# Moving the second-half query work and the routing tables inside two narrow attentions of a four-layer transformer kernel

## The reference

```
x = x + xattn0(LN(x), ctx)    # 8 heads of 16        "a0"
x = x + moe0(LN(x))           # top 2 + shared       "f0"
x = x + xattn1(LN(x), ctx)    # 8 heads of 128       "a1"
x = x + moe1(LN(x))           # top 2                "f1"
x = x + xattn2(LN(x), ctx)    # 16 heads of 8, mask  "a2"
x = x + moe2(LN(x))           # top 2                "f2"
x = x + xattn3(LN(x), ctx)    # 16 heads of 8, bias  "a3"
x = x + moe3(LN(x))           # top 1                "f3"
```

## Time and profile before

| | us |
|---|---|
| median of 3 executions (lowest, highest) | 915.8 (913.2, 916.91) |
| profiled execution, its time | 914.47 |
| profiled execution, its span | 912.7 |
| PE busy | 747.1 (82%) |
| DVE busy | 483.6 (53%) |
| ACT busy | 374.2 (41%) |
| POOL busy | 138.8 (15%) |
| mean granted TensorE clock, share of full speed | 0.903 |

### The profile page before, as it was taken

The page is one execution under the profiler, slowest core; times in us unless marked ns, Lnnn a source line. Parts: engine busy times, 40 slices in busy tenths (PEclk is TensorE's granted clock), DMA queues, the critical chain, the costliest instruction groups (busy, mean ns, idle before and its releaser), DMA issues.

```text
span 912.7 us, 14542 instructions
## 1 busy us (share of the span) xinstructions
PE 747.1 (82%) x5219; PEld 575.4 (63%) x5219; DVE 483.6 (53%) x1477; ACT 374.2 (41%) x768; POOL 138.8 (15%) x282
## 2 busy tenths in 40 slices
PE   3157899999998998799398936999999995898367
PEld 2025588887774666689387813676798982454266
DVE  6355574353325558766755325665655436576423
ACT  1024654433334554553243303556443331565234
POOL 7021130000000001013500001111000003123124
PEclk9568999999999999989799957999999996799679
DMA  4729930001254545990003623113001531323253
GB/s 118 137 37 277 152 95 1 1 24 50 63 179 137 164 159 150 206 202 10 1 1 72 68 34 57 52 52 98 1 1 46 73 56 33 50 77 86 71 152 153
DMA packets 78164, 77.49 MB, mean 85 GB/s; under 512 B 10849, under 2 KB 69237, under 8 KB 78094
## 3 DMA queue, kind: packets, MB, share of 16 engines
q1 hardware_dynamic: 77230, 74.99, 37.0%
q0 software_dynamic: 864, 1.58, 0.5%
HBM read 46.65 MB, written 28.78 MB: 83 GB/s over the span
## 4 chain that ended last, share of the span: by engine, by line
PE 60%; DVE 15%; DMA 11%; SPq 4%; issue 4%; POOL 3%; ACT 2%; POOLq 0%; DVEq 0%; ACTq 0%
PE bank L1692 15%; PE bank L1424 13%; PE bank L1512 4%; DMA big<-parts_scratch 4%; DVE xn L620 3%; PE bank L1495 3%; PE bank L1460 3%; DMA parts_scratch<-big 3%; SPq L344 3%; PE bank L1776 3%; PE bank L1809 2%; DMA big<-nmT 2%; PE bank L1651 1%; PE bank L1676 1%; DVE x_res L977 1%
## 5 line engine op out<-in xcount | busy, mean ns | idle before, releaser
L1692 PEld LDWEIGHTS bank<-W,late 128*128 128x128 f32 x1600 | 185.8, 192 | 8.3 <-issue 4.1
L1692 PE MATMUL bank<-W,late 128*128 128x128 f32 x1600 | 186.5, 275 | 0.0
L977 DVE SCALAR_TENSOR_TENSOR x_res<-bank,comb,x_res 128x128 f32<-128x128 f32 x200 | 56.3, 344 | 167.5 <-PE bank L1692 165.8
L1266 ACT ACTIVATE late<-bank,b 128x512 f32<-128x512 f32 x136 | 91.9, 688 | 95.2 <-PE bank L1424 94.3
L742 DVE TENSOR_REDUCE negmax<-bank 128x2 f32<-128x512 f32 x128 | 85.6, 689 | 84.2 <-PE bank L1460 56.6
L1460 PE MATMUL bank<-big 128*128 128x256 bf16 x320 | 74.4, 310 | 55.1 <-DMA big<-parts_scratch 42.5
L1424 PE MATMUL bank<-nH,wH 128*128 128x512 f32 x200 | 88.9, 445 | 2.5 <-DVE nL L780 2.4
L1195 ACT ACTIVATE late<-bank 128x512 f32<-128x512 f32 x120 | 70.6, 594 | 48.3 <-PE bank L1500 22.3
L1495 PE MATMUL bank<-big 128*128 128x256 bf16 x320 | 76.7, 290 | 11.9 <-DMA big<-nmT 10.2
L1460 PEld LDWEIGHTS bank<-big 128*128 128x128 bf16 x320 | 29.5, 107 | 84.9 <-issue 53.2
L1424 PE MATMUL bank<-nH,wL 128*128 128x512 f32 x200 | 81.3, 407 | 0.0
(11 more groups left out here) (269 smaller groups left out, 1278.2 us busy)
## 6 DMA issues: line engine op xcount, KB each, us to landing
W<-in_f_w SPq DMA_DIRECT2D x50, 256.0 KB, 3.5
rows_scratch<-zrow SPq DMA_DIRECT2D x1, 9252.0 KB, 54.4
late<-bands_scratch SPq DMA_DIRECT2D x8, 1024.0 KB, 5.8
big<-parts_scratch SPq DMA_DIRECT2D x18, 256.0 KB
big<-parts_scratch SPq DMA_DIRECT2D x36, 128.0 KB
W<-in_f_wx SPq DMA_DIRECT2D x8, 512.0 KB, 3.8
big<-in_f_wx SPq DMA_DIRECT2D x7, 578.0 KB, 6.9
bands_scratch<-late SPq DMA_DIRECT2D x3, 1276.0 KB, 6.6
```

What stands on the lines that cost most here:

```text
L977: ins = v.scalar_tensor_tensor(x[:, t, :], bank[4 + u % 2][:, 128 * i:128 * (i + 1)], comb[:, t, e:e + 1], x[:, t, :], ALU.mult, ALU.add)
L1266: ins = a.activation(dst, bank[c][:, :], func, bias=b1[:, bi, FC * e + c:FC * e + c + 1])
L1692: ins = mm(dst[:, 128 * i:128 * (i + 1)], hid[u % 2][:, c, 128 * i:128 * (i + 1)], W[:, e, F + 128 * c:F + 128 * (c + 1)], start=c == 0, s ...
```

## The change

The steps of the second half of the queries are tied to SECOND_HALF: unchanged for a0 (1), for a2 and a3 statistics in step 12, scaling in 13, transposes and matmul in 15, parts in 18. SyncE stores the second half ahead of the maxima of group 4 and loads it behind them. Experts are loaded one behind each of groups 6 to 13. On GpSimd the maxima parts of groups 0 to 2 go ahead of the layer norm a2.1 or a3.1. The tables are built after the layer norm f2.1, inside the mixture f2, and the row numbers (two iotas) apart from them, before the first rows are sent.

```diff
+SECOND_HALF = {"a0": 1, "a2": 12, "a3": 12}
...
                 stack(key, 0, 0)
-                maxima_to_rows(key, 0)
-                stack_out(key, 0, 1)
-                maxima_to_rows(key, 1)
-                stack_in(key, 0, 1)
-                for g in range(2, 16):
+                for g in range(16):
+                    if g == 4:
+                        stack_out(key, 0, 1)
                     maxima_to_rows(key, g)
-                    if g >= 4 and g % 2 == 0:
-                        expert(nxt, g // 2 - 2)
-                for e in range(6, 8):
-                    expert(nxt, e)
+                    if g == 4:
+                        stack_in(key, 0, 1)
+                    if g >= 6:
+                        expert(nxt, g - 6) if g < 14 else None
...
-            def route_tables():
+            def row_numbers():
 
                 pool.wait_ge(*at("f2", "down", 16))
                 pool.wait_ge(*at("f1", "acc", 16))
...
                 for hf in range(2):
                     ins = pool.iota(sends[hf][:, :, 2 * D:ROWW].bitcast(i32), pattern=[[128, 4], [0, 1]], base=512 * hf, channel_multiplier=1)
                 ins.then_inc(sem("f3.ids"), 1)
+
+            def route_tables():
+
+                pool.wait_ge(*at("f1", "acc", 16))
...
             for name in norms:
                 if name == "a1.0":
                     wide_tables()
+                if name in ("a2.1", "a3.1"):
+                    maxima_parts(name[:2], range(3))
                 layer_norm_rstd(name)
...
-                if name in ("a0.1", "a2.1", "a3.1"):
-                    maxima_parts(name[:2], range(0, 8 if name == "a0.1" else 2))
-                if name == "a3.1":
+                if name == "a0.1":
+                    maxima_parts("a0", range(8))
+                if name == "f2.1":
                     route_tables()
                 if name in ("a2.1", "a3.1"):
-                    maxima_parts(name[:2], range(2, 13))
+                    maxima_parts(name[:2], range(3, 13))
                 if name in ("f2.0", "f3.0"):
                     maxima_parts(BEFORE[name[:2]], range(13, 16))
+                if name == "f3.0":
+                    row_numbers()
...
+                start = SECOND_HALF[key]
...
-                    if i == 1:
+                    if i == start:
                         x_ready(dve, key, 1)
                         norm_stats(key, 1, x)
-                    if i == 2:
+                    if i == start + 1:
                         norm_apply(key, 1, x, xn)
-                    if i == 7:
+                    if i == start + 6:
                         query_parts(key, 1)
...
-                    if i == 4:
+                    if i == SECOND_HALF[key] + 3:
                         copy_T(key, 1, nT[0])
                         queries(key, 1)
...
-                    if i == 4:
+                    if i == SECOND_HALF[key] + 3:
                         turn_norm(key, 1)
                         queries(key, 1)
```

## The result

| | before | after |
|---|---|---|
| median of 4 executions (lowest, highest), us | 916.36 (913.2, 921.35) | 905.5 (905.16, 908.19) |
| profiled execution, span, us | 912.7 | 903.9 |
| mean granted TensorE clock | 0.903 | 0.913 |

The account below looks back on a forecast made before the run. The prediction took the attentions' steady parts as full, with starts waiting on second-half work, tables and maxima transfers. Gains of 4.0 us (a2) and 1.0 (a3) took the median from 915.8 to 910.8 us, range 904 to 918.

Parts of the forecast that it names:

- Step 11 after a start without query work: Start of a2 and a3: without second-half work step 11 comes earlier, 6.4 us gained in a2 and 7.7 in a3.
- The assumed flight of the first maxima: Start of both attentions: transfer takes 2.5 to 3 us, no wait; at 4.8 us both starts lose together 4.3.
- The moved work in the full part: Query work put into steps 12 to 18: costs 3.9 us in a2 and 7.7 in a3.
- The stop moves: PE's wait for maxima moves from step 19 to step 31: stops of 5.5 us in a2 and 7.6 in a3.
- The tables: Start of a3: building them in f2 takes PE's 2.81 us wait out of the path to step 16.
- Low clock behind the stop: After the stop in step 31 PE runs at a low clock, losing 1.0 us in a2 and 1.3 in a3.
- Sum: Both attentions up to step 31: gain of 4.0 us in a2 and 1.0 in a3, 5.0 in total.
- the one for spread: Whole-kernel median: 0.5%, 4.6 us, taken as about what a measurement can tell from no change.
- rival 1: Second-half loads run better mid-attention, landing in 9 us, not 14: 899 to 901, half of it 905; chance 0.13.
- An even trade: Moved work costs in the steady part all it cost in the start, stop hides nothing: 913.3 us; chance 0.25.
- The clock: PE stays at 1.2 GHz over eleven steps of a2 and six of a3: 13 us, giving 924; chance 0.12.

Follow-up runs that it names:

- Run 1: Kernel before with only the routing tables moved into the third mixture, queries and transfers as before: 913.82 us, ratio 0.9994 to the kernel before.
- run 6: Changed kernel without the six second-half loads of a2 and a3, output not the reference's: 892.19 us, ratio 0.9783 to the kernel before.
- The larger comparisons: Changed kernel unaltered, timed twice more beside the kernel before: 910.05 against 915.69 us, ratio 0.9931; 907.93 against 912.54 us, ratio 0.9963.
- run 5: Changed kernel with second-half queries computed in steps 1 to 7 again, transfers still late: 914.31 us against 911.97 before, ratio 1.0012.
- versions 8 and 9: Changed kernel, loads two by two: 8 with query work from step 8, behind groups 3-5, 901.06 us; 9 from step 12, behind groups 4-6, 907.13 us.
- run 7: Changed kernel with the six second-half loads issued on ScalarE's queue in step 22: 905.68 us against 911.97 before, ratio 0.9946.
- version 10: Changed kernel with query work from step 8 and loads two by two on ScalarE's queue in steps 18, 22, 26: 898.16 us, ratio 0.9871 to before.

## Why the prediction was right, and where it was off

**Step 11 after a start without query work.** Forecast 10.0 us (a2) and 7.9 (a3) from the first scores; measured 9.4 and 7.85. Right, with a2 paced slightly faster than 0.85 a step. The assumed flight of the first maxima, 2.5 to 3 us, also held: issued at 754.30 in a3, and PE took up step 11 at 757.03 without a wait, so at most 2.7. The 2.0 us that the prediction names from the Trainium skill (DMA: Bandwidth & Descriptors, Anatomy of one DMA) are stated there for transfers that GpSimd issues; for SyncE's there is only this bound, which neither confirms nor contradicts them.

**The moved work in the full part.** Forecast, from step 11 to step 22, 17.4 us in a2 and 17.9 in a3; measured 15.8 (546.62 to 562.43) and 16.5 (757.03 to 773.51). This term was sized too high in this execution by 1.6 and 1.4. In a2 of the changed kernel's second profile it was 17.4 (27.0 less 9.6), as forecast, and in a3 of its third 17.5, so the price itself moves by up to 1.6 us between executions. The clock moves with it: in that second profile the query matmuls and what follows them were granted 0.57 for 4 us, and the two matmuls took 1.87 us, where the first profile has a clock of 1.00 and 1.10 us. PE's wait for ScalarE's copy does not move: 0.78 in all fourteen profiles.

```profile
554.40:558.40 4.00, 3.67 (x14) 1.71 (x18) 1.14 (x5) 0.84 (x3) 0.78 (x4) 0.57 0.00 0
```

**The stop moves.** Forecast: 16.1 us (a2) and 15.7 (a3) from turning group 4 to the restart, stops of 5.5 and 7.6. Measured 16.14 and 15.74, stops of 5.71 and 7.78; in the two other profiles of the same kernel 6.45 and 8.52, 4.85 and 7.88, with 16.9 and 16.5, 15.3 and 15.8 us from turning to restart. This was the best part of the forecast, and the match to 0.1 us is luck of the first profile. It came from two rows of before, and holds because the six loads set the landing, wherever they stand: 13.6 to 15.3 us behind their issue in these three profiles.

**The tables.** Costed inside the sum for a3 as 2.81 us taken out of the path to step 16, with the landing behind the loads as the last word on the end. Run 1 shows that this was the right way to count: alone they are worth nothing.

**Low clock behind the stop.** Forecast 1.0 us (a2) and 1.3 (a3), a quarter of some 4.4 and 4.8 us at 1.2 GHz. This term was sized too low. PE took up step 31 at 41.3 us after the first scores of a2, where the kernel before has 48.4: 7.0 us ahead. At the second group of 16 matmuls behind the stop it was 4.7 ahead. In a3 it was 40.1 against 43.7, 3.6 ahead, and then 1.2. So 2.3 and 2.4 us were lost there, and the distance to run 6 over the same stretch gives nearly the same. The windows shown with run 6 make 5.0 and 6.0 us at 1.2 GHz of it (an estimate from 0.72 and 0.59, with full speed for the rest), and PE lost not a quarter but over 0.4 of that.

**Sum.** Forecast 4.0 + 1.0. The first pair of traces shows 4.7 in a2 and, up to the second group behind the stop, 1.2 in a3. That these come so near is in part luck: PE was ahead at step 31 by 7.0 and 3.6 us where the sum had 5.0 and 2.3, mostly because the moved work cost less, and the low clock took back 1.3 and 1.1 us more than the sum had. At the end of a3 it is 2.2. Of the 2.2, 1.2 stand by group 5 and 1.0 comes at group 11, near step 57: there the kernel before ran its transposes and scores at a clock of 0.88, the changed one at 1.00 (windows 820:834 and 813:827). That was not in my sum, and it does not belong to the change: run 1, with the queries as before, has 6.1 us for that stretch like the changed kernel's first profile, and the second profile of the changed kernel has 7.1 like the kernel before.

**The median.** 10.9 instead of 5.0 us. The forecast set the sum against a median 1.3 above the profiled execution and took 0.5% as what can be told apart. The larger comparisons, 5.6 and 4.6 us by medians, agree with 5.0; the term that failed is the one for spread, which I had as a single bound and not as several us on either median. That 905.5 lies inside the range of 904 to 918 says little for the mechanism: it is near the lower end, where the range had put rival 1, and rival 1 is not what happened.

**The rivals.** Loads that run better in the middle: no, 14.5 and 14.2 us. An even trade: run 5 shows that it is true of the late transfer, and nearly true of the query work in a3 (0 to 1.4 us saved by step 22), but not in a2 (2.5 to 4.4). The clock: in the first profile the steps up to 22 of a2 ran at full speed (granted 1.00 from 542.67 to 562.43), in the second some 4 us of them at 0.57, beside the 1.6 us above; in a3 the first profile has 0.72 from 763.00 to 769.00, around the query matmuls, which the forecast for a3 had allowed for. So the rival came true for a few us and not over the steps that it needed. One reading against it was wrong: PE was not at the full clock from 553.86 on in the kernel before, but fell back within a microsecond:

```profile
554.85:558.40 3.55, 3.55 (x20) 2.63 (x19) 2.04 (x7) 1.42 (x3) 0.78 (x4) 0.57 0.41 121
```

## What to carry to other kernels

A start that waits on latency and a steady part that is full are two different places: work of the same length can be cheaper in the second, as in a2; in a3 it was nearly an even trade. VectorE had less slack there (busy 25.67 of 34.60 us against 28.29 of 44.00); that this makes the difference was not tested. Before counting a wait as a gain, ask what ends last behind it; 2.81 us of visible idle were worth nothing because a transfer landed later than they ended. A block of transfers ahead of a short one in its queue cost about the same wherever it stood. Dividing it and starting it four steps earlier was together worth twice the change studied here; dividing it alone was worth nothing. A stop costs more than its own length: behind 5.7 and 7.8 us of idle PE lost 2.3 and 2.4 us more at the low clock.

## What was not expected of the hardware

- Two loads of 128 KB, the last pair of six, took 6.0 to 6.2 us from their issue on SyncE's queue until PE could use them in a2 and 8.1 to 8.8 in a3 (versions 8 and 9), where I had reckoned 4; what stood around them in the queues is part of that. Behind six in one block the next maxima were usable 13.6 to 15.3 us after the first load's issue.
- Six loads in another queue still held up a 24 KB transfer: in run 7 PE went on 7.7 and 8.1 us after its issue, with stops of 2.8 and 4.4 us, where the first such transfer of an attention was usable within 2.7.
- Before the first scores of a2, in code that no version changed, PE was idle for 9.15 to 18.24 us in the fourteen profiles, ended by the keys' and first queries' loads. The first scores of a2 came at 533.7 to 543.4 us, while the stretch between the two attentions took 115.2 to 118.0 and the tail behind a3 64.5 to 66.5. So this stretch is the likeliest source of the spread of the medians; it was not taken apart further.

```profile
543.40 0.37 PE L1481 MATMUL bank<-big 128*128 128x256 bf16 x1 [18.24 <-DMA big<-parts_scratch]
```

```profile
533.67 0.37 PE L1474 MATMUL bank<-big 128*128 128x256 bf16 x1 [9.15 <-DMA big<-parts_scratch]
```

The first is the version with a2 alone (without it the longest is 17.56), the second is version 10.
